# Attention scores of two kinds, interleaved product by product over the four row groups of TensorE

## The reference, cut to what matters

```python
scores = jnp.einsum('bhqd,bhkd->bhqk', q, k) / jnp.sqrt(jnp.asarray(dh, x.dtype))
if mask is not None:
    scores = jnp.where(mask[:, None, :, :], scores, jnp.asarray(-1000000000.0, x.dtype))
attn = jax.nn.softmax(scores, axis=-1)
out = jnp.einsum('bhqk,bhkd->bhqd', attn, v)
```

## Time and profile before

| | |
|---|---|
| median of 3 runs | 498.4 us (497.85 to 498.58) |
| the profiled execution | 498.25 us |
| its span in the trace | 496.4 us |
| PE busy | 426.7 us (86%), 5646 matmuls |
| DVE busy | 363.7 us (73%) |
| ACT busy | 270.3 us (54%) |
| mean granted TensorE clock | 0.962 of full |
| S and T products, as recorded | 512 + 512, 220 and 219 ns each, busy 26.0 + 25.4 us |

### The profile page before, as it was taken

One profiled execution on the slowest core, in us unless ns is written; L12 is line 12 of the kernel. 1 busy time (PEld: TensorE's weight loads), 2 busy tenths in 40 slices (PEclk: granted clock), 3 DMA queues, 4 the chain that ended last, 5 costly groups with the idle time before them and its releaser, 6 DMA issues.

```text
span 496.4 us, 14119 instructions
## 1 busy us (share of the span) xinstructions
PE 426.7 (86%) x5646; PEld 278.9 (56%) x5646; DVE 363.7 (73%) x906; ACT 270.3 (54%) x399; POOL 163.8 (33%) x297
## 2 busy tenths in 40 slices
PE   1898788889769999878888887698798999999996
PEld 0555456555336666456565655555454647776775
DVE  5475567778798888557868688655656783999995
ACT  1411455552647767256666565343444576777862
POOL 7003234212358886443323333213224011121110
PEclk9999799998999999979999999879979989999999
DMA  7000000000011132000000000000000001112101
GB/s 260 7 1 12 12 18 18 19 2 1 16 34 49 48 98 77 2 1 3 3 2 3 3 1 3 1 24 2 23 3 1 1 2 44 44 54 76 42 1 44
DMA packets 9066, 13.10 MB, mean 26 GB/s; under 512 B 1450, under 2 KB 7474, under 8 KB 9010
## 3 DMA queue, kind: packets, MB, share of 16 engines
q1 hardware_dynamic: 9012, 12.32, 8.0%
HBM read 11.79 MB, written 0.52 MB: 25 GB/s over the span
## 4 chain that ended last, share of the span: by engine, by line
PE 58%; DVE 24%; POOL 6%; ACT 6%; issue 4%; DMA 1%; DVEq 0%; POOLq 0%; ACTq 0%
DVE smax L1374 8%; PE bk L904 5%; PE sc L846 4%; PE bk L897 3%; PE bk L1227 3%; PE bk L1217 3%; PE bk L1219 3%; PE sc L1077 3%; PE sc L1078 3%; PE sc L1079 3%; DVE inv_sum L1389 2%; PE bk L948 2%; PE bk L880 2%; POOL rstd L415 2%; PE sc L833 2%
## 5 line engine op out<-in xcount | busy, mean ns | idle before, releaser
L1374 DVE TENSOR_REDUCE smax<-sc 128x8 f32<-128x1024 f32 x64 | 78.1, 1220 | 62.3 <-PE sc L846 62.0
L619 ACT ACTIVATE probs<-sc 128x1024 f32<-128x1024 f32 x64 | 65.1, 1025 | 62.8 <-PE sc L846 62.7
L1707 DVE SCALAR_TENSOR_TENSOR x_all<-bk,comb,x_all 128x128 f32<-128x128 f32 x192 | 53.7, 344 | 1.4 <-PE bk L1227 1.3
L541 POOL TENSOR_TENSOR gated_lo<-gated,gated_hi 128x512 f16<-128x512 f32 x36 | 41.7, 1160 | 28.8 <-ACT gated_hi L700 27.5
L735 ACT ACTIVATE probs<-sc,w 128x512 f32<-128x512 f32 x64 | 41.1, 687 | 16.6 <-PE sc L1079 16.5
L897 PE MATMUL bk<-probs,v_pad 128*32 128x128 f32 x1024 | 39.1, 298 | 3.7 <-issue 2.4
L413 POOL TENSOR_SCALAR ln_var<-mv 128x2 f32<-128x2 f32 (+1 forms) x18 | 4.5, 250 | 110.3 <-DVE mv L1277 110.1
L1785 DVE TENSOR_TENSOR p_lo<-probs,p_hi 128x1024 f16<-128x1024 f32 x32 | 38.4, 1223 | 3.4 <-ACT p_hi L742 2.8
L449 POOL TENSOR_TENSOR w_lo<-w,w_hi 128x1024 f16<-128x1024 f32 x8 | 18.0, 2248 | 61.6 <-ACT w_hi L615 61.6
L904 PE MATMUL bk<-probs,ones_pad 128*32 128x128 f32 x1024 | 37.2, 290 | 0.0
L634 ACT ACTIVATE qkT<-bk 128x1024 f16<-128x1024 f16 x32 | 32.6, 1020 | 7.9 <-PE bk L825 7.9
(11 more groups left out here) (254 smaller groups left out, 1071.1 us busy)
## 6 DMA issues: line engine op xcount, KB each, us to landing
w<-in_w SPq DMA_DIRECT2D x8, 514.0 KB, 3.5
w<-in_w SPq DMA_DIRECT2D x18, 192.0 KB, 2.3
wd<-in_wd SPq DMA_DIRECT2D x1, 644.0 KB
x_all<-in_x SPq DMA_DIRECT2D x1, 512.0 KB, 4.1
ctxT<-in_ctx_t SPq DMA_DIRECT2D x4, 128.0 KB, 3.3
ctx_tok<-in_ctx SPq DMA_DIRECT2D x4, 128.0 KB, 2.2
mask_in<-in_mask SPq DMA_DIRECT2D x4, 128.0 KB, 2.5
out<-x_all SPq DMA_DIRECT2D x1, 512.0 KB, 3.2
```

The source lines that it names most:

```text
L541: pool.tensor_tensor(gated_lo[:, k % DEPTH, :], gated[:, k % DEPTH, :], gated_hi[:, k % DEPTH, :], ALU.subtract).then_inc(c_glo, 1)
L619: act.activation(probs[:, n % 2, half, :], sc[half][:, :], ACT.Exp, scale=HD ** -0.5).then_inc(u_exp, 1)
L1374: dve.tensor_reduce(smax[:, s, 8 * half:8 * half + 8], sc[half][:, :].rearrange("p (h k) -> p h k", k=S), X, ALU.max).then_inc(u_max, 1)
L1707: op = dve.scalar_tensor_tensor(x_all[:, bb, :], (bk4, bk5)[k % 2][:, b * 128:(b + 1) * 128], w, x_all[:, bb, :], ALU.mult, ALU.add)
```

## The change

The helper `heads` is gone. `score` and `score_T` issue one product, `masks` the mask matmuls of one half, and `scores` takes both halves of a call: S of (p, s, half) and, where there is one, T of (q, t, 1 - half). All waits of both come first, with one exception: the masks of S are issued before T's own waits. Then come the masks of T, and then the products in turns: two of S (row groups of one half), two of T (row groups of the other half), four times. Both semaphores are raised at the end. In calls 2 and 4 S now comes first. A call without a partner is as before.

```diff
-            def heads(p, s, half, rows, stationary, moving, swap):
-
-                mask = p.kind == "given"
-                if mask:
-                    for jj in range(2):
-                        mask_pass(sc[half][:, jj * 512:(jj + 1) * 512], mask_b[:, p.i % 2, s, :], swap)
-                for g in range(G):
-                    for jj in range(2):
-                        r = slice(32 * (2 * half + jj), 32 * (2 * half + jj) + rows)
...
-            def scores(p, s, half):
+            def wait_scores(p, s, half):
...
+            def wait_scores_T(q, s, half, more):
+
                 n = q.n + s
                 pe.wait_ge(u_qmT, n + 1)
                 if half == 0 and more:
                     pe.wait_ge(u_max, 2 * n + 3)
...
+            def scores(p, s, half, q=None, t=0):
+
+                wait_scores(p, s, half)
+                if p.kind == "given":
+                    masks(p, s, half, False)
+                if q:
+                    wait_scores_T(q, t, 1 - half, True)
+                    if q.kind == "given":
+                        masks(q, t, 1 - half, True)
+                for g in range(G):
+                    for jj in range(2):
+                        mm = score(p, s, half, jj, g)
+                    if q:
+                        for jj in range(2):
+                            tt = score_T(q, t, 1 - half, jj, g)
+                mm.then_inc(u_s, 1)
+                if q:
+                    tt.then_inc(u_st, 1)
...
                 if p:
-                    scores(p, 0, 0)
+                    scores(p, 0, 0, q, 1)
+                elif q:
+                    scores_T(q, 1, 1)
                 if p and not q:
                     keep_busy(bank_d, 7)
-                if q:
-                    scores_T(q, 1, 1, p)
...
-                if q:
-                    scores_T(q, 1, 0, p)
+                if p:
+                    scores(p, 0, 1, q, 1)
+                elif q:
+                    scores_T(q, 1, 0)
...
-                    scores(p, 1, 0)
-                    scores_T(p, 0, 1, True)
+                    scores(p, 1, 0, p, 0)
...
-                    scores_T(p, 0, 0, True)
-                    scores(p, 1, 1)
+                    scores(p, 1, 1, p, 0)
```

More of the change, by code:

```diff
@@ L835, in mask_pass @@
                     pe.matmul(wide, ident_b[:, :], mask.unsqueeze(1).to_broadcast([128, G, S]), start=True, stop=True)
-            def heads(p, s, half, rows, stationary, moving, swap):
-                mask = p.kind == "given"
-                if mask:
-                    for jj in range(2):
-                        mask_pass(sc[half][:, jj * 512:(jj + 1) * 512], mask_b[:, p.i % 2, s, :], swap)
-                for g in range(G):
-                    for jj in range(2):
-                        r = slice(32 * (2 * half + jj), 32 * (2 * half + jj) + rows)
[L846 to L849, removed]
-            def scores(p, s, half):
+            def wait_scores(p, s, half):
                 n = p.n + s
-                rows = SPLIT_ROWS + BITS if p.kind == "segment" else SPLIT_ROWS
                 pe.wait_ge(u_qkT, n + 1)
@@ L862, in scores @@
                     pe.wait_ge(u_exp, 2 * n - 1)
-                heads(p, s, half, rows, lambda r, g: qkT[r, s, g, :], lambda r, g: qkT[r, s, 4 + g, :],
-                      False).then_inc(u_s, 1)
-            def scores_T(q, s, half, more):
+            def wait_scores_T(q, s, half, more):
                 n = q.n + s
@@ L870, in scores_T, with masks, score, score_T @@
                     pe.wait_ge(u_max, 2 * n + 3)
-                heads(q, s, half, SLOT, lambda r, g: qkT[r, s, 4 + g, :], lambda r, g: qmT[r, s, g, :],
-                      True).then_inc(u_st, 1)
+            def masks(p, s, half, swap):
+                for jj in range(2):
+                    mask_pass(sc[half][:, jj * 512:(jj + 1) * 512], mask_b[:, p.i % 2, s, :], swap)
+            def score(p, s, half, jj, g):
+                rows = SPLIT_ROWS + BITS if p.kind == "segment" else SPLIT_ROWS
+                r = slice(32 * (2 * half + jj), 32 * (2 * half + jj) + rows)
+                mask = p.kind == "given"
+                return pe.matmul(sc[half][:, jj * 512 + g * 128:jj * 512 + (g + 1) * 128], qkT[r, s, g, :],
+                                 qkT[r, s, 4 + g, :], start=not mask, stop=True, skip_group_check=mask)
+            def score_T(q, s, half, jj, g):
+                r = slice(32 * (2 * half + jj), 32 * (2 * half + jj) + SLOT)
+                mask = q.kind == "given"
+                return pe.matmul(sc[half][:, jj * 512 + g * 128:jj * 512 + (g + 1) * 128], qkT[r, s, 4 + g, :],
+                                 qmT[r, s, g, :], start=not mask, stop=True, skip_group_check=mask)
+            def scores(p, s, half, q=None, t=0):
[10 more added lines that the diff above has]
+                    if q:
+                        for jj in range(2):
+                            tt = score_T(q, t, 1 - half, jj, g)
+                mm.then_inc(u_s, 1)
+                if q:
+                    tt.then_inc(u_st, 1)
+            def scores_T(q, s, half):
+                wait_scores_T(q, s, half, False)
+                if q.kind == "given":
+                    masks(q, s, half, True)
+                for g in range(G):
+                    for jj in range(2):
+                        tt = score_T(q, s, half, jj, g)
+                tt.then_inc(u_st, 1)
             def stack_maxima(p, s, following):
@@ L1103, in stage @@
                     keep_busy(bk5[:, :], 4)
-                if p:
-                    scores(p, 0, 1)
                 if r:
```

## The result

The changed kernel takes 495.4 us (median of 5 runs, 493.0 to 496.47) against 498.58 for the kernel before (5 runs beside them, 497.85 to 499.15): a ratio of 0.993, 95% interval 0.9911 to 0.9948. It is faster by 0.7%, and outside the range of the prediction. The profiled execution of after, 493.0 us with a span of 491.2, is the fastest of its five, so its span is 5.2 us shorter than that of before where the medians differ by 3.2.

The account below looks back on a forecast made before the run. The chain of waits was taken as the bound, TensorE holding 58%. Masked terms of -0.1 and unmasked +0.2 gave +0.1 us on the profiled 498.25, so 498.35; with 0.15 to the median, 498.5 us, range 496.4 to 500.6.

Parts of the forecast that it names:

- Unmasked calls: The 44 merged calls that touch no mask: 0 in calls 1 and 3, small delays elsewhere, together +0.2 us.
- The masked call: Calls with both masks in A to D: each saves 0.41 us of TensorE, but the half that came first is late.
- The terms outside the low clock: Masked-stage terms apart from call 2 of A and C: -0.11, +0.24, -0.11, +0.28, +0.28 and -0.37 us.
- A3 to B1: From call 3 of stage A to call 1 of B: calls 3 and 4 of A gain, -0.11 us.
- B3 to C1: From call 3 of stage B to call 1 of C: call 4 of B gains, -0.11 us.
- Call 2 of A and C: Call 2 in masked stages A and C, worked at the lower clock: about -0.1 us in A, -0.23 in C.
- The clock rival: Masked stages: the number of stretches at the lower clock changes, 2.1 us a stretch, either way; chances 0.13 and 0.09.
- one fewer: One stretch at the lower clock fewer: 496.4 us, chance 0.09.
- one more: One stretch at the lower clock more: 500.6 us, chance 0.13.
- The gain arrives: Rival, masked calls: with more cover behind the exponential, TensorE's 5.7 us count in full, 492.8 us at best; chance 0.10.
- Products in program order: Rival, all 60 merged calls: S and T did not overlap before, saving 12.6 us, 485.9 at best; chance 0.02.
- The late exponential: Rival, ScalarE in masked calls: exponential up to 0.20 us later still, together 1.6 us, so 500.1; chance 0.14.

Follow-up runs that it names:

- E2: Changed kernel with only the 44 unmasked calls merged and the masked calls in the old order: 500.03 us, ratio 1.0006.
- F1: Kernel before with seven filler matmuls ahead of `stack_T` in every masked stage, no merged call: 494.0 us, ratio 0.9919.
- G4: Kernel before with seven filler matmuls ahead of `stack_T` in stage C alone: 495.3 us, ratio 0.993.
- F2: Changed kernel with seven filler matmuls ahead of `stack_T` in every masked stage: 494.69 us, ratio 0.9923.
- H2: Changed kernel with seven filler matmuls ahead of `stack_T` in stages A and C alone: 494.23 us, ratio 0.9905.
- H3: Kernel before with seven filler matmuls ahead of `stack_T` in stages A and C alone: 494.56 us, ratio 0.9919.
- E4: Kernel before with five more filler matmuls (23 for 18) ahead of the first attention: 499.18 us, ratio 1.0009.
- F4: Changed kernel with only masked calls 1, 3 and 4 merged; call 2 and unmasked calls as before: 499.38 us, ratio 1.0006.
- E1: Changed kernel with only the calls of masked stages A to D merged, the 44 unmasked calls in the old order: 495.16 us, ratio 0.993.
- E3: Changed kernel with eight S and then eight T in program order instead of in turns: 496.71 us, ratio 0.996.
- F3: Changed kernel with only call 2 of the masked stages merged, all other calls as before: 494.37 us, ratio 0.9915.
- G2: F3 with T's wait and masks ahead of S's in call 2: 494.5 us, ratio 0.9932.
- H1: Changed kernel with 23 filler matmuls for 18 ahead of the first attention: 495.77 us, ratio 0.9936.
- G1: Kernel before with S ahead of T in call 2 of the masked stages, still apart: 497.49 us, ratio 0.9981.

## Why the prediction was wrong

**Unmasked calls, 0 (+0.2): right.** From 224 to 307 us, in the long and segment stages, the maxima of after start 0.30 to 0.16 us ahead of those of before, a lead that the start of the program left; so the calls cost 0.14 us at most. E2 agrees within its interval.

**The masked call: right.** With t0 = 363.36: maximum at +1.40 (forecast 1.41), exponential at +1.45 (1.50), TensorE free at +1.30 (1.33); call 4's first mask at +2.61 behind the exponential of call 3 (2.66), its maximum at +4.01 (4.07), its exponential at +4.05 (4.16). `stack_maxima` of C then waits for the copy `qkT`, at +6.13 for 5.96 before: +0.17, forecast +0.28.

**The terms outside the low clock: right in sum, one in sign.** A3 to B1 -0.16 (forecast -0.11); B1 to B3 +0.17 (+0.24); B3 to C1 +0.16 (-0.11: the path goes through `stack_maxima` there as it does in C); C3 to D1 and D1 to D3 +0.16 each (+0.28 each); D3 to the first expert product -0.43 (13.10 for 13.53 us; forecast -0.37). Together +0.06 against +0.21.

**Call 2 of A and C, -0.1 and -0.23: the step that failed.** C's was worked out at a granted clock of 0.50 up to the value products, because rows 6 show that, and A's by the same working. The clock was taken as part of the stage, where it was an outcome of what TensorE does there. The segments that hold these terms went down by 2.31 us (A1 to A3) and 2.14 (C1 to C3). F1 and G4 show that the clock alone can do this: without a merged call, with the wait filled, the same segments go down by 1.93 and 2.09 in F1, and C's by 2.10 in G4. What calls 1 and 2 are worth at the higher clock, F2 against F1 shows in A (8.15 for 8.16, so nothing) and H2 against H3 in C (9.09 for 9.74, so 0.65, which B and D, +0.17 and +0.16, and the ways between them take back for the most part). So in C about 1.5 of the 2.14 us are clock, by difference.

**The clock rival: price right, weight and number wrong.** A stretch was priced at 2.1 us, and G4 measured 2.10. But "one fewer" had 0.09 beside "one more" with 0.13, as if chance decided. In the profiles, kernels with call 2 of the masked stages as it stood, and no fillers, always took 62.15 to 62.62 us from A1 to D3 (before, E2, E4, F4), kernels with it merged 58.3 to 59.8 (after, E1, E3, F3, G2, H1); the shifts of E4 and H1 changed neither. Behind `stack_T` of A and C, the first four were low for 6.8 us in all eight places; the other six for 3.4 us in nine of twelve and not at all in three (A of after, C of F3 and of H1). So the edit itself shortens both stretches at least by half; which of them go altogether differs from kernel to kernel, and there chance has its part. That a new wait of TensorE would cost clock was also argued from the wrong call: the new waits of 0.69 us in calls 3 and 4 cost none, and the wait that mattered, ahead of `stack_T`, was there all along.

**The gain arrives, 492.8: the right direction, the wrong reason.** The median is 495.4. The saved 5.7 us of TensorE are for the most part spent waiting, as the prediction had it; H3 reaches the time of the changed kernel without saving any. **Products in program order** fell with E3. **The late exponential** fell with +1.45.

What stays open is why the clock comes back sooner. In the first 3.4 us of the low stretch TensorE was busy for 3.29 us in before and 3.31 of 3.45 in after; in before it held two mask pairs and 16 products in two runs, with 0.3 us left for the value products, in after a part of the masks, 16 products in one run and 1.95 us of value products, as this timeline of after shows:

```profile
357.43 0.40 PE L823 MATMUL bk<-ident_h,q_stack 128*128 128x128 f16 x4 [2.39 <-POOL k_stack L506]
...
357.89 0.59 PE L835 MATMUL sc<-mask_b,ident_b 128*128 128x512 bf16 x2
358.32 1.00 PE L833 MATMUL sc<-ident_b,mask_b 128*128 128x512 bf16 x2
...
359.80 2.21 PE L929 MATMUL bk<-probs,v_pad 128*32 128x128 f32 x32
```

The value products start 1.91 us behind the first mask; before, 363.00 - 360.01 = 2.99. Where in the call the clock falls does not decide it. In E3 it fell at 359.97 us, 0.13 ahead of the first mask of call 2 in C, and in before 0.11 ahead of it (359.90); yet E3 was back after 3.4 us:

```profile
360.00:363.35 3.35, 3.35 (x40) 1.52 (x37) 2.08 (x4) 0.66 (x1) 1.85 (x2) 0.50 0.02 5
363.40:366.80 3.40, 2.83 (x60) 1.74 (x56) 0.86 (x3) 1.82 (x3) 1.40 (x4) 1.00 0.00 0
```

The stretches hardly differ in TensorE's busy time either, and which property of the work counts was not separated: G1, with the order alone, and G2, with the products alone, each shorten the stretch.

## What to carry to other kernels

Where a profile shows a stretch at the lower clock, its length is not a given: ask of every edit in it, or just behind the wait that precedes it, whether it packs TensorE's work more closely, and price the stretch from the same work at the two clocks (here 7.04 against 4.95 us). Before such an edit is credited with its work, fill the wait with matmuls that nobody reads; if that alone gives the gain, as here, the clock was the bound. Put fillers only where TensorE waits: seven of them cost up to 1.36 us in the one stage that had no wait.

## What the runs showed of the hardware

Three things are worth keeping. The granted clock came back after about half the low time (3.45 us for 6.8) when call 2 was packed more closely. Matmuls on different row groups start out of program order by several places: in E3 the first two T start 0.02 us after the first two S, ahead of six S that stand before them. And the place of low stretches outside the change (around 52 to 65, 96 to 126, 307 to 312 and 400 to 426 us) differs from execution to execution of nearly the same program, which spread the spans ahead of A1 over 3.3 us and those behind D3 over 3.5: a difference of single profiled executions says little of a change of 1%, where the stretch that it touches says much.
